# Local attention with its four engine orders written anew: bias product a beat later, values of two pairs at once, maxima in the bank of the sums

## The reference, cut to what matters

```python
shifted = jnp.roll(x, (-SS, -SS), axis=(1, 2))
win = shifted.reshape(B, H_ // WS, WS, W_ // WS, WS, C).transpose(0, 1, 3, 2, 4, 5).reshape(-1, N, C)   # N = 64
qkv = (win @ qkv_w.T + qkv_bias).reshape(-1, N, 3, NH, hd).transpose(2, 0, 3, 1, 4)                     # NH = 16, hd = 8
attn = jnp.einsum('bhnd,bhmd->bhnm', _l2n(q), _l2n(k)) * scale + rpb[None]      # then the window mask
attn = jax.nn.softmax(attn, axis=-1)
out = jnp.einsum('bhnm,bhmd->bhnd', attn, v).transpose(0, 2, 1, 3).reshape(-1, N, C)
out = out @ proj_w.T + proj_b
x = x + _ln(out, norm1_g, norm1_b)
```

## Time and profile before

| | |
|---|---|
| Median of 3 runs | 3876.11 us (3854.44 to 3879.24) |
| Profiled execution, its own time | 3907.29 us |
| Its span, first to last instruction | 3905.5 us |
| Mean granted TensorE clock over the span | 0.803 |
| PE, weight loads, DVE, ACT, POOL busy over the span | 83%, 60%, 62%, 41%, 29% |

### The profile page before, as it was taken

How to read it: one execution, slowest core, us unless ns; L and a number is a source line. 1 busy time by engine, 2 the same in 40 slices (tenths; PEclk the granted TensorE clock), 3 DMA queues, 4 the chain that set the end, 5 groups by cost and what they waited for, 6 DMA issues and landing times. The chain is left out here.

```text
span 3905.5 us, 96986 instructions
## 1 busy us (share of the span) xinstructions
PE 3235.1 (83%) x35431; PEld 2362.5 (60%) x35431; DVE 2413.6 (62%) x6510; ACT 1589.2 (41%) x3175; POOL 1141.7 (29%) x1360
## 2 busy tenths in 40 slices
PE   2888888888886997999888888887884799988887
PEld 1565565656554775777787655665663466655555
DVE  2555555555554555888687776666664577766666
ACT  1444444444443442343300332332331577766665
POOL 0222222222222331111000155554556000035555
PEclk9656555565555998999998987777775899999999
DMA  2000000000000221000000011111111344432222
GB/s 85 15 17 16 16 17 16 17 16 17 17 16 21 68 73 39 22 21 21 6 4 4 26 44 39 43 40 37 42 33 46 94 95 98 94 84 76 78 77 72
DMA packets 298397, 162.23 MB, mean 42 GB/s; under 512 B 98300, under 2 KB 289160, under 8 KB 297736
## 3 DMA queue, kind: packets, MB, share of 16 engines
q1 hardware_dynamic: 281608, 123.16, 11.7%
q0 software_dynamic: 16384, 33.59, 2.9%
HBM read 66.74 MB, written 71.30 MB: 35 GB/s over the span
## 5 line engine op out<-in xcount | busy, mean ns | idle before, releaser
L2302 DVE TENSOR_TENSOR e_glo<-e_g,e_ghi 128x512 f16<-128x512 f32 x540 | 373.5, 692 | 250.2 <-ACT e_ghi L2209 201.1
L2204 ACT ACTIVATE e_g<-psum,b 128x512 f32<-128x512 f32 x540 | 370.3, 689 | 285.9 <-PE psum L2358 236.3
L2375 PE MATMUL psum<-w2hi,e_ghi 128*128 (+1 forms) x2160 | 399.1, 221 | 72.6 <-DVE e_glo L2302 62.8
L2188 POOL DMA_INDIRECT e_got<-ys_dram,e_idx x256 | 252.0, 984 | 609.2 <-DMA ys_dram<-e_yo 421.4
L2379 PE MATMUL psum<-w2hi,e_glo 128*128 (+1 forms) x2160 | 394.3, 220 | 6.9 <-issue 6.8
L2377 PE MATMUL psum<-w2lo,e_ghi 128*128 (+1 forms) x2160 | 393.9, 220 | 0.2
L2375 PEld LDWEIGHTS psum<-w2hi,e_ghi 128*128 128x128 f16 x2160 | 211.9, 98 | 211.4 <-issue 98.9
L592 DVE TENSOR_TENSOR pT<-pT,rpbx 128x512 f32<-128x512 f32 x128 | 90.0, 703 | 356.3 <-ACT pT L544 356.3
L1737 POOL DMA_INDIRECT xs_dram<-m_xt,m_idxl x256 | 262.9, 1027 | 114.4 <-issue 72.3
L479 POOL TENSOR_TENSOR rstd<-mv,eps 128x1 f32<-128x1 f32 x128 | 24.5, 191 | 824.8 <-DVE mv L637 824.8
L586 DVE TENSOR_REDUCE mx<-psum 128x16 f16<-128x1024 f32 x128 | 156.1, 1219 | 126.3 <-PE psum L663 126.1
(11 more groups left out here) (332 smaller groups left out, 8018.8 us busy)
## 6 DMA issues: line engine op xcount, KB each, us to landing
ys_dram<-e_yo SPq DMA_DIRECT2D x71, 256.0 KB
f_xm<-x_dram SPq DMA_DIRECT2D x32, 256.0 KB
mid_dram<-f_xm SPq DMA_DIRECT2D x32, 256.0 KB
l_t<-mid_dram SPq DMA_DIRECT2D x16, 512.0 KB
m_t<-mid_dram SPq DMA_DIRECT2D x16, 512.0 KB
res_dram<-m_rest SPq DMA_DIRECT2D x16, 512.0 KB
e_acc<-res_dram SPq DMA_DIRECT2D x32, 256.0 KB
out_dram<-e_acc SPq DMA_DIRECT2D x32, 256.0 KB
```

The costliest lines, as they stand in the source:

```text
L2188: gp.indirect_dma_start(out=got[:, q % 2, k, t, :], out_offset=None, in_=ys, in_offset=bass.IndirectOffsetOnAxis(idx[:, q // 2, i:i + 1], 0))\
L2204: ac.activation(g32[:, c % 4, :], bank(c % 4), ACT.Gelu, bias=bias, scale=1.0 / WSCALE)\
L2302: ve.tensor_tensor(glo[:, c % 4, :], g32[:, c % 4, :], ghi[:, c % 4, :], ALU.subtract)\
L2375: pe.matmul(o, ghi[:, c % 4, g], w2hi[:, e, f, :], start=first and t == 0, stop=False, skip_group_check=True)
```

## The change

*PE.* Beat s is now: scores s+1; in an even beat the transposes of q and k (s+2), the output's transpose (s-2), the input's transposes (now of the unit of s+6); in an odd beat the output's transpose, the q and k products and all values of the unit of s+5; then in every beat the projection of s-2, the transpose of the maxima of s+1, the turned scores of s, the sums of s-1. The maxima go to the last 64 columns of bank 7, the bank of the sums; `sums` waits for their copy (`mT_ok` of q+2).

*Values.* Once per unit, 8 matmuls of a window's 64 tokens against 64 columns each, to one half of the partitions each (before: 4 matmuls of 128 by 128). `xT` holds each window once. The host sorts the value weights by the parity of the head.

*ACT.* The maxima's copy stands before the second two masked copies in an even beat and right behind `onT` in an odd one; values are copied once per unit, in two instructions of 64x256 instead of four of 64x128, at the end of the odd beat; `xT` is 128x256 instead of 128x512, at the end of the even beat.

*DVE.* The bias product of half 2:4 is that of pair s-1 and stands before the maxima. `x1` is gone from DVE.

*POOL.* Order: x plus bias (s+4), bias product (s), rstd (s-2), and `x1` of s-2 in two instructions (h1 times rstd, plus x1), each of them 128x128.

*SP.* Loads are those of pair s+10, stores those of s-2. Pieces as before. The loops start at -6 instead of -5.

```diff
-                for s in range(-5, NP * NB + 4):
+                for s in range(-6, NP * NB + 4):
...
-                        load(s + 8)
-                        q = s - 3
+                        load(s + 10)
+                        q = s - 2
...
+                            met(gp, rstd_ok, q)
+                            met(gp, xb_ok, q)
+                            met(gp, h_ok, q)
+                            apart(gp)
+                            gp.tensor_tensor(h1[:, q.odd, :], h1[:, q.odd, :], rstd[:, k:k + 1].to_broadcast([P, C]), ALU.mult)                                .then_inc(hr_ok.sem, 1)
+                            met(gp, hr_ok, q)
+                            gp.tensor_tensor(x1[:, q.p, :], x1[:, q.p, :], h1[:, q.odd, :], ALU.add).then_inc(x1_ok.sem, 1)
...
+                    def even(s):
...
+                        turned_out(s - 2)
+                        masked(q, 0)
+                        masked(q, 1)
+                        turned_maxima(s + 1)
+                        masked(q, 2)
+                        masked(q, 3)
+                        exponential(s)
+                        q = s + 6
+                        if q.real():
+                            unit(ac, xT_ps, q)
+                            unit(ac, v_ps, q - 4)
+                            ac.activation(xT[:, q.u % 2].rearrange("p w t -> p (w t)"), bank(5)[:, 0:2 * P], ACT.Copy)\
+                                .then_inc(xT_ok.sem, 1)
...
+                        q = s - 1
+                        if q.real():
+                            met(ve, pr_ok, q, 2)
+                            p = pT[:, q.odd, 2:4]
+                            e = bias[:, 2:4].unsqueeze(2).to_broadcast([P, 2, 2, 2 * N])
+                            ve.tensor_tensor(p, p, e, ALU.mult).then_inc(pd_ok.sem, 1)
...
                             met(ve, mv_ok, q)
+                            met(ve, x1_ok, q - 2)
...
-                        met(pe, v_ok, q)
+                        unit(pe, v_ok, q)
                         met(pe, on_ok, q - 1)
+                        met(pe, mT_ok, q + 2)
...
+                            for w in range(4):
+                                for k in range(2):
+                                    i = pe.matmul(bank(5)[half(k), 256 + N * w:256 + N * w + N], xT[:, q.u % 2, w, :],
+                                                  wqkT[:, 2 * C + 64 * k:2 * C + 64 * k + 64], start=True, stop=True)
+                            i.then_inc(v_ps.sem, 1)
+
+                    def beat(s):
+                        if (s + 1).real():
+                            scores(s + 1)
+                        if s.odd:
+                            odd(s)
+                        else:
+                            even(s)
+                        project(s - 2)
+                        q = s + 1
+                        if q.real():
+                            met(pe, mx_ok, q)
+                            met(pe, mT_ok, q - 1)
+                            met(pe, on_ok, q - 3)
+                            pe.transpose(bank(7)[:, 448:512].bitcast(F16), mx2[:, q.kind(), :], ident16[:]).then_inc(mT_ps.sem, 1)
+                        if s.real():
+                            turned_scores(s)
+                        q = s - 1
+                        if q.real():
+                            sums(q)
```

More of the change, by code:

```diff
@@ L497, in _ @@
                 def _(ac):
[L498 to L507, removed]
                     def masked(q, g):
@@ L513, in masked, with turned_out @@
                                           bank(4)[:, 0:2 * P].rearrange("p (a w t) -> p a w t", a=2, w=2), ACT.Copy, scale=msk[:, g:g + 1]).then_inc(qm_ok.sem, 1)
[L515 to L532, removed]
+                    def turned_out(q):
                         if q.real():
@@ L536, in beat, with turned_maxima @@
                             ac.activation(onT[:, q.odd, :], bank(6)[:, 0:P], ACT.Copy).then_inc(onT_ok.sem, 1)
[L537 to L548, removed]
+                    def turned_maxima(q):
                         if q.real():
@@ L567, in _, with exponential @@
-                    beats(ac, beat)
+                            ac.activation(mT[:, q.odd, :], bank(7)[:, 448:512].bitcast(F16), ACT.Copy).then_inc(mT_ok.sem, 1)
+                    def exponential(q):
+                        if q.real():
+                            met(ac, t_ps, q)
+                            met(ac, o_ps, q - 2)
+                            for f in range(2):
+                                ac.activation(pT[:, q.odd, 2 * f:2 * f + 2].rearrange("p j w n -> p j (w n)"), turned[:, 2 * f:2 * f + 2],
+                                              ACT.Exp).then_inc(pr_ok.sem, 1)
@@ new lines, in odd @@
+                    def odd(s):
+                        turned_out(s - 2)
+                        turned_maxima(s + 1)
+                        q = s + 5
+                        if q.real():
+                            unit(ac, qk_ps, q)
+                            unit(ac, tr_ps, q - 4)
+                            ac.activation(qk[:, q.u % 2].rearrange("p a k c -> p (a k c)"), bank(4), ACT.Copy)\
+                                .then_inc(qk_ok.sem, 1)
+                        exponential(s)
+                        if q.real():
+                            unit(ac, qk_ok, q)
+                            unit(ac, ss_ok, q - 2)
+                            ac.activation(sq[:], qk[:, q.u % 2].rearrange("p a k c -> p (a k c)"), ACT.Square)\
+                                .then_inc(sq_ok.sem, 1)
+                            unit(ac, v_ps, q)
+                            met(ac, o_ps, q - 7)
+                            for k in range(2):
+                                half = slice(64 * k, 64 * k + 64)
+                                i = ac.activation(vd[half, q.u, :, :, k, 0:HD],
+                                                  bank(5)[half, 256:512].rearrange("p (w h d) -> p w h d", w=4, d=HD), ACT.Copy)
+                            i.then_inc(v_ok.sem, 1)
@@ L569, in _ @@
+                    beats(ac, lambda s: odd(s) if s.odd else even(s))
                 @block.vector
@@ L699, in sums, with out_first, project, even @@
                         i.then_inc(o_ps.sem, 1)
-                    def value_rows(q):
+                    def out_first(q):
                         if q.real():
[L704 to L714, removed]
+                            met(pe, on_ok, q)
+                            met(pe, h_ok, q - 1)
+                            pe.transpose(bank(6)[:, 0:P], on[:, q.odd, :], ident[:]).then_inc(onT_ps.sem, 1)
+                    def project(q):
+                        if q.real():
+                            met(pe, onT_ok, q)
+                            pe.matmul(bank(6)[:, P:2 * P], onT[:, q.odd, :], projT[:], start=True, stop=False)
+                            pe.matmul(bank(6)[:, P:2 * P], ones16[0:64, :], pb2[:], start=False, stop=True)\
+                                .then_inc(pj_ps.sem, 1)
+                    def even(s):
                         q = s + 2
-                        if not s.odd and q.real():
+                        if q.real():
                             unit(pe, qn_ok, q)
@@ L723, in beat @@
                             i.then_inc(tr_ps.sem, 1)
[L724 to L728, removed]
+                        out_first(s - 2)
+                        q = s + 6
+                        if q.real():
                             landed(pe, q)
                             landed(pe, q + 1)
-                            met(pe, v_ok, q - 1)
-                            met(pe, mT_ok, s)
+                            unit(pe, v_ok, q - 2)
                             for a in range(2):
```

95 lines of the change are left out of this document (26 added, 69 removed).

## The result

The changed kernel takes 3669.0 us (median of 4 runs, 3649.5 to 3687.5) against 3873.3 for the one before: a ratio of 0.948, 95% interval 0.941 to 0.955. Run again on another chip the ratio was 0.947 (0.943 to 0.951). The forecast was 3702, in a range of 3655 to 3800.

What follows compares the result with a forecast made beforehand. PE bounds the kernel: 14.5 us of steps plus 0.27 and 0.15 of waits make 14.9, plus 0.2 gives 15.1 a unit for 17.84; 174 us less, 3702 us. Own range 3670 to 3735, overall 3655 to 3800.

Steps and rivals of the forecast that it cites:

- 5.95 + 0.15 + 0.2: PE's even beat: 5.95 us of steps, up to 0.15 waiting for ACT's `onT`, 0.2 for DVE's late bias product.
- the wait for `onT` (0.15): PE's projection waits for ACT's `onT`, which stands behind `kT`: up to 0.15 us.
- the port (0.2): DVE's bias product meets GpSimd operations and can take double, coming late for the even beat's maxima: 0.2 us added.
- 8.53 + 0.27: PE's odd beat: 8.53 us of steps plus 0.27 waiting for the quotient before the output's transpose.
- the sums' row: Profile row of PE's sums, 32 records alternating between two halves at 0.057 us each; basis for values at 1.0 us.
- rival A: Upper clock lets PE run ahead and SP's DMA issues bind: 14.7 us a unit, 199 us less, 3677; chance 0.20.
- The unknown clock hardly moves my number: Without the upper clock the unit is 15.1 us; with it throughout, SP's 14.7 binds, only 0.4 us apart.
- SP's floor: SP's DMA issues, 58.8 us an image or 14.7 us a unit, as the next bound.
- B: New waits eat half: values cost 2.0 us, bias product 0.9 late in the even beat; unit 16.8, 3810; chance 0.15.
- C: No gain: a copy ahead of one PE needs in ACT's order costs 2 to 3 us; 3840 to 3915; chance 0.07.
- D: Slower: POOL waits for landed stores, delaying its bias product and the sums; 80 us more, 3956, at L = 12; chance 0.05.
- a sign that I had named for being wrong: POOL (GpSimd) waiting for stores, listed among the signs that the forecast is wrong; no size given.

Runs made afterwards that it cites:

- experiment 3: Changed kernel with loads spread over three queues (SP half, ACT and GpSimd a quarter each): ratio 0.948 to the kernel before, unit 14.66 us.
- experiment 1: Changed kernel with its 8 value matmuls of a unit issued twice: ratio 0.941 to the kernel before, unit 14.43 us.
- experiment 8: Three-queue loads, even beat's input transposes moved ahead of the sums: ratio 0.964; with value matmuls twice 0.925; in both places with values twice 0.910.
- experiment 6: Changed kernel with DVE's bias product back behind the maxima, for the pair of the same beat: ratio 1.049, units of 21.39 us.
- experiment 5: Changed kernel with ACT's copy of the maxima behind the exponential in both beats: ratio 1.000 to the kernel before, unit 18.01 us.

## Why the prediction was right

**The bound and its sum.** The forecast's term was PE at the lower clock, 15.1 us; the units at that clock take 15.38. Even beat: 5.95 + 0.15 + 0.2 = 6.30 forecast, 6.30 measured, and that agreement is luck. Neither the wait for `onT` (0.15) nor the port (0.2) is in the unit; in their place the stretch of projection, maxima and turned scores takes 2.4 us in its new order for my 2.19, and the three transposes of output and input take 0.85 for my 0.69. Odd: 8.53 + 0.27 = 8.80 forecast, 9.08 measured. There the same stretch is 0.2 longer (2.39, 705.96 to 708.35), the wait for the quotient 0.43 by starts for my 0.27, values and output's transpose 0.1 longer together, and the q and k products 0.17 shorter (2.78 for 2.95). Values: 1.0 forecast from the sums' row, 1.05 measured, so the two halves do run beside each other.

**The clock.** I took none of the upper one. The changed kernel was granted it in a few units, which lowers the mean from 15.38 to 14.89 (14.72 in the second run). So two misses work against each other: the unit at the lower clock is 0.28 longer than my 15.1, 18 us in the phase, and the clock gives 31 us back. Together they are 13 of the 33 us by which the total came out under 3702. The other 20 are outside of the units: the median of before is 3873 where I started from 3876, and the medians of the two kernels are 204 us apart where 63.5 times the units' difference is 187. That the total lies in the range owes something to this. It landed near rival A's 3677, but A's mechanism is not what ran: units are not 14.5 but 15.38, with shorter ones between them, the mean clock from 400 to 1000 us is 0.56 and not over 0.7, PE waits neither for loads nor for GpSimd's product, and with SP relieved (experiment 3) the mean stays. A mean near a floor does not show that the floor binds. A became true only in experiment 1, where the clock was up.

**"The unknown clock hardly moves my number"** rested on SP's floor, 0.4 us below my unit. In the changed kernel the floor was hardly put to the test, since the clock was mostly the lower one; in experiment 1, with the clock up, it did hold the unit at 14.4 to 14.7. It holds only as long as SP has 20 DMAs a unit: with SP relieved and the clock at 0.89 to 0.96, a unit takes 12.06 us (experiment 8) instead of 15.38, the largest gain that any edit here showed.

**The port.** I added 0.2 us for DVE's product meeting GpSimd's operations. The wrong part was the timing: its median is 681 ns, and 681 with `x1` back on DVE. In the unit shown GpSimd's product ends 0.3 us before DVE's starts (701.41 and 701.72), DVE's meets only the rstd steps, and the `x1` steps start (702.40) as it ends. Where the two products do meet, the price is full. In 18 of the changed kernel's 128 beats, 12 of them while the upper clock is granted, DVE's product takes 890 to 1717 ns, and each time it ends 0.54 to 0.55 us behind the end of GpSimd's, however early it started. In experiment 6 it is so in every beat, and in the fastest kernel of experiment 8, at the upper clock, it takes over 800 ns in 68 of 128 (median 979). The Trainium skill (SBUF — State Buffer, SBUF: two separate sides) has this as an exclusive lock; the trace agrees there. Beside the rstd steps, which are 128x1, nothing is lost (100 beats at a median of 681): no number here shows why.

**Stalls removed.** The order of the copy of the maxima is worth the 3.2 us that experiment 5 takes back, and the later bias product 6.0 us in this order. They don't add up to the change: each is a need of the new order, not a share of the gain. Nor was any part of the change put into the kernel before by itself. As work the values are 0.95 us less (2.00 to 1.05); in the timelines the upper clock that the unit of before had and the one of 15.38 lacks costs about as much, so the gain of the 15.38 unit is the size of the stalls. What the shorter values would have brought alone was not tried.

**Rivals.** B did not come: values at 1.05 us and not 2.0, and no wait for a late bias product in the even beat. C did not come: PE has no wait there for a copy of ACT's. D did not either, though a sign that I had named for being wrong did come, GpSimd waiting for stores. Its loop is real: GpSimd waits 102 us in 600 for landed stores, nearly all of it covered at 15.38 us a unit, and it becomes PE's wait at 11.

## What to carry to other kernels

Work out the cost of issuing DMAs as a bound of its own, pieces times issue time, beside the engines' shares: here it was 82% of the phase before and appeared in no busy share. Read a phase unit by unit before explaining a mean; 14.9 was a mixture of 15.38 and 11.6 to 13.9, and the floor of 14.5 beside it did not make it. Before moving an instruction, look at what it covers: two transposes that filled a wait cost 0.63 us elsewhere. Where PE is busy at the lower clock, a test with repeated matmuls tells cheaply whether a denser order would be granted the upper one, and what binds next if it is.

## What the runs showed that I had not expected

- Doubling 1.05 us of matmuls in each unit took the granted clock from 0.60 to 0.78 (400 to 600 us) and made the phase of the profiled executions 18 to 29 us shorter. The Trainium skill (TensorE: Matmul & The Clock Gate, What's actually happening) says that activity releases the throttle. The trace agrees only in part: the repeated work did bring the clock up, but PE of the changed kernel was 98% busy from 800 to 1000 us at 0.50, and with the repeated values it was busy 82% of 400 to 600 us at 0.78.
- The same two transposes ahead of the sums lost 0.63 us a unit when moved there without the second values, and gained 1.3 when issued there in addition with them (13.37 to 12.06, or 13.43 to 12.06 against the moved ones on the same chip).
- Every unit of before had the upper clock around its stall, which saved it some 0.9 us; 48 of 63 units of the changed kernel lack it, and that used up what the shorter values saved.
- A clock record can be missing: 1.00 shown for 200 to 400 us, with every matmul at the duration of 0.50.
